# A Mamba and mixture-of-experts layer on one core: experts' copies and Silu ahead of the unit's Silu and softplus, norms turned a step later, routing operands in PSUM

## The chip, the cores and the metric

One core of a Trainium2 chip runs the kernel. The metric is the device time in microseconds (us) of one execution. The kernel before was timed three times: 1050.92, 1051.12 and 1053.75 us, median 1051.12. One further execution was profiled; all rows below are from it.

## The reference

The input x is 8 batches of 512 tokens of width 128. It is normalised once (`xn`), and the output is x plus two branches of `xn`:

```python
x = x + attn_ref(xn, ...) + ffn_ref(xn, ...)
# attn_ref: xn2 = layernorm(xn); for each direction d in (f, b):
xi, z = split(xn2 @ in_w.T);  xi = silu(conv4(xi) + conv_b)
dt, Bm, Cm = split(xi @ x_w.T, [8, 24])
delta = softplus(dt @ dt_w.T + dt_b)
h = h * exp(delta * A) + (delta * xi) * Bm      # 512 steps, 256 channels x 16 states
y = (sum(h * Cm) + xi * D) * silu(z);  out_d = y @ out_w.T
# attn = concat(out_f, out_b) @ combine_w.T + combine_b + xn
# ffn_ref: each token goes to expert e = argmax(xn @ router_w.T), of 8 experts
g = xe @ gate_w[e].T; u = xe @ up_w[e].T; ye = (silu(g) * u) @ down_w[e].T   # 352 wide
```

## The kernel before

**Units and steps.** A unit is one batch in one direction, so there are 16 units (`UNITS`). A unit has 16 steps (`NSTEP`), and 256 steps (`LAST`) make the scan; a few more follow. Each engine has its own program, and each program walks the same step numbers m in a loop written out by hand. What an engine does in a step stands in the order of the source. Engines meet through semaphores only, so a wait in one engine's step holds everything that stands behind it on that engine.

**The scan.** DVE does in an even step the product with B (`du_B`, line 997, 2048 elements a partition) and in the following odd step the linear recurrence (`scan`, lines 1015 and 1017). For the product of step m+1, PE first spreads `delta*xi` over partitions into `in_b` (`spread_du`, line 553); this stands first in PE's odd step m, behind all of PE's step m-1. ACT makes the decays `dA` four steps ahead (`decay(m + LEAD)`, line 847). POOL multiplies by C (line 1246), PE sums the states into the bank Y seven and eight steps later (`sum_states`, line 577).

**The front of a unit.** The projections of unit v are made during the unit before it, at fixed distances from its first step 16v. On PE: `in_proj` at -16 to -13, `x_proj` at -11, `dt_proj` at -10 and -9, `z_proj` at -7 and -6. On ACT: `keep_xi(v,0)` at -14; at step 16v-12, here called the Silu step, the load of the Silu table, `keep_xi(v,1)`, `silu(v)` (lines 791 and 794, xi of unit v and z of unit v-1) and the load of the exp table; `dbc_out` at -10; `dt_out` and `softplus` at -9 and -8; `keep_z` at -6 and -5. `x_proj` waits for the Silu, `dt_proj` for `dbc_out`. Softplus is computed as two activations of the exp and ln set; Silu lives in another set, and every change of set is a load of a table on ACT. Copies, Identity, Relu and Abs run under either set.

**Norms and routing.** In steps -3 to 26, ACT normalises the batches (`norm_one(c)` at 3c), PE turns each (`turn_xn`, 3c+2), ACT copies it out of the bank M (`turned_xn`, 3c+3), PE makes the router's logits in M (`router`, 3c+4) and ACT keeps them (`keep_logits`, 3c+5). `turn_xn(c)` waits until `keep_logits(c-1)` has left M. In step 27 (`R0`) DVE runs `route()`, 21 small instructions between a product with B and its recurrence: argmax by comparison, a prefix count with one pair of PE matmuls in the middle, positions and the expert of each tile. After it POOL scatters the tokens (32 indirect DMAs, steps 30 to 46).

**Experts.** 39 tiles of 128 sorted tokens follow, one each 3.75 steps, in steps 44 to 204 (`tiles_at(m, k)` gives the tiles whose stage k falls in step m). Per tile: PE gate matmuls (k=8, line 702) and the turn of the next tile; ACT at k=9 loads the Silu table (line 938), makes `th_f` = silu(gate) (line 943), loads the exp table (line 944) and copies `xsT` (line 948); PE at k=10 does the down matmuls of two tiles ago (line 634) and the up matmuls (line 639); ACT at k=11 copies `up_f` and, for two tiles ago, `ys` (lines 927 and 932). The gate matmuls wait for `up_f` of the tile before and for `ys`. In the tail, from step 207, POOL gathers the experts' rows back (32 indirect DMAs).

The Silu steps of units 1 to 16 are 4, 20, 36, ..., 244. Stage k=9 of a tile falls in the Silu steps 68, 116 and 180, and in the step after it for 52, 100 and 164. Stage k=11 falls in the Silu steps 100 and 148. ACT reads and refills the bank Y (`next_y`, lines 825 and 829) in steps with m % 8 = 5, that is also in the step after every Silu step.

## Time and profile before

| what | us |
|---|---|
| median of 3 executions | 1051.12 |
| the profiled execution | 1057.89 |
| its span in the trace | 1054.4 |
| DVE busy | 902.9 (86%) |
| POOL busy | 831.8 (79%) |
| PE busy | 812.2 (77%) |
| ACT busy | 741.2 (70%) |
| mean granted clock of TensorE | 0.887 of full speed |

Times in the rows count from the start of the span. A timeline row gives start, duration, engine, source line, operation and, in brackets, how long the engine had been idle before it and what ended that; "issue" means that the trace shows no releaser. PEld is the loading of weights beside the matmuls.

### The profile page before, as it was taken

Reading aid. Unit: us, or ns where it says so; the run is one execution under the profiler, and the core shown is the slowest. Engines: PE = TensorE matmul, PEld = TensorE weight load, DVE = VectorE, ACT = ScalarE, POOL = GpSimd, SP = SyncE. Lnnn points to the kernel's source line nnn. Section 1 sums busy time; section 2 is a strip of 40 time slices with the busy share of each in tenths; the row PEclk is TensorE's granted clock in tenths of the full one; section 3 lists DMA queues with packets and bytes.
Section 4 is the critical chain, followed back from the end, with each engine's and each line's share of the span. In section 5 each row is a group of like instructions: output and inputs, shape, how many; then the busy total and the mean of one; then the engine's idle time right before and its main releaser. Section 6 shows DMA issues by size and latency. Waiting matters only on the chain. (4 is left out here: it accounts for less than half of the span.)

```text
span 1054.4 us, 10031 instructions
## 1 busy us (share of the span) xinstructions
PE 812.2 (77%) x2887; PEld 326.5 (31%) x2887; DVE 902.9 (86%) x370; ACT 741.2 (70%) x1179; POOL 831.8 (79%) x474
## 2 busy tenths in 40 slices
PE   5777856755888897878988897887988887675556
PEld 2322311122233433424333443424324231112112
DVE  4789799956899988978999897977989999999696
ACT  3877744715798879797899879878888858465420
POOL 0288657889987969768797978877787889999992
PEclk9868997887899999899999998989989999788787
DMA  5676260252444526344364545433264433425200
GB/s 185 175 227 157 70 183 21 83 160 70 134 142 117 152 73 190 92 146 108 85 187 110 159 109 155 128 136 102 76 178 95 136 83 111 107 64 167 72 5 10
DMA packets 91303, 125.50 MB, mean 119 GB/s; under 512 B 8041, under 2 KB 62698, under 8 KB 87154
## 3 DMA queue, kind: packets, MB, share of 16 engines
q1 hardware_dynamic: 88464, 120.15, 40.4%
q0 software_dynamic: 2048, 4.20, 1.3%
q10 hardware_dynamic: 738, 0.53, 0.2%
q8 instruction: 23, 0.38, 0.1%
q14 instruction: 30, 0.25, 0.1%
HBM read 75.44 MB, written 16.38 MB: 87 GB/s over the span
## 5 line engine op out<-in xcount | busy, mean ns | idle before, releaser
L1246 POOL TENSOR_TENSOR hs<-hs,C_rep 128x1024 f32<-128x1024 f32 x253 | 593.3, 2361 | 186.6 <-DVE hs L1015 105.5
L847 ACT ACTIVATE dA<-delta_rep,A_sb 128x511 f32<-128x511 f32 x512 | 335.6, 715 | 83.7 <-DVE hs L1017 46.0
L997 DVE TENSOR_TENSOR in_b<-in_b,B_rep 128x2048 f32<-128x2048 f32 x128 | 294.3, 2299 | 108.1 <-PE in_b L553 92.7
L577 PE MATMUL y<-hs,cst 128*32 128x512 f32 x1024 | 277.4, 674 | 56.4 <-POOL hs L1246 56.4
L1015 DVE TENSOR_TENSOR_SCAN hs<-dA,in_b 128x2048 f32<-128x2048 f32 x64 | 282.9, 4421 | 8.5
L1017 DVE TENSOR_TENSOR_SCAN hs<-dA,in_b 128x2048 f32<-128x2048 f32 (+1 forms) x65 | 283.0, 4355 | 8.3
L553 PE MATMUL in_b<-du,cst 128*128 128x512 f32 x256 | 155.7, 696 | 25.4 <-DVE hs L1017 22.5
L515 PE MATMUL front<-xpad,w_in 128*128 128x512 f32 x248 | 125.3, 630 | 11.2 <-ACT xi L778 7.2
L577 PEld LDWEIGHTS y<-hs,cst 128*32 128x32 f32 x1024 | 55.9, 120 | 245.9 <-issue 195.5
L778 ACT ACTIVATE xi<-front,cols 128x512 f32<-128x512 f32 x30 | 20.6, 687 | 79.0 <-PE front L515 79.0
L553 PEld LDWEIGHTS in_b<-du,cst 128*128 128x128 f32 x256 | 46.1, 209 | 93.9 <-issue 91.7
L515 PEld LDWEIGHTS front<-xpad,w_in 128*128 128x128 f32 x248 | 44.7, 196 | 82.4 <-issue 65.4
L634 PE MATMUL moe<-dn_w,th_f 128*128 128x128 f32 x234 | 38.0, 304 | 36.2 <-issue 36.2
L546 PE MATMUL front<-dbc,w_dt 8*128 8x512 f32 x62 | 40.4, 735 | 25.3 <-ACT dbc L801 25.2
L634 PEld LDWEIGHTS moe<-dn_w,th_f 128*128 128x128 f32 x234 | 33.3, 209 | 62.7 <-issue 62.7
L944 ACT ACT_TABLE_LOAD x39 | 50.0, 1283 | 0.7
L528 PE MATMUL front<-xpad,w_in 128*128 128x512 f32 x62 | 36.0, 664 | 18.1 <-ACT zs L784 18.0
L938 ACT ACT_TABLE_LOAD x36 | 46.2, 1283 | 0.6
L825 ACT COPY yg<-y 128x512 f32<-128x512 f32 x31 | 17.8, 574 | 35.8 <-PE y L577 35.8
L702 PE MATMUL moe<-xsT,gu_w 128*128 128x128 f32 x234 | 37.0, 298 | 7.3 <-ACT ys L932 7.3
L702 PEld LDWEIGHTS moe<-xsT,gu_w 128*128 128x128 f32 x234 | 32.8, 205 | 30.0 <-issue 30.0
L639 PE MATMUL moe<-xsT,gu_w 128*128 128x128 f32 x234 | 36.5, 298 | 7.0 <-ACT xsT L948 7.0
(131 smaller groups left out, 845.2 us busy)
## 6 DMA issues: line engine op xcount, KB each, us to landing
delta_rep<-tmpA SPq DMA_DIRECT2D x126, 256.0 KB, 4.4
B_rep<-dbc_scratch SPq DMA_DIRECT2D x16, 1024.0 KB, 5.1
C_rep<-dbc_scratch SPq DMA_DIRECT2D x16, 1024.0 KB, 7.4
gu_w<-in_gate_up SPq DMA_DIRECT2D x39, 384.0 KB, 3.5
dn_w<-in_down SPq DMA_DIRECT2D x39, 192.0 KB, 2.4
xs<-sorted_tokens SPq DMA_DIRECT2D x39, 64.0 KB, 3.0
sorted_ffn<-ys SPq DMA_DIRECT2D x39, 64.0 KB, 1.6
sorted_tokens<-up_f SPq DMA_DIRECT2D x9, 256.0 KB, 3.6
```

What stands on the lines that cost most here:

```text
L515: i = e.matmul((M if v == 0 and h else F)[:, :], w_in[:, d, k, h * P:(h + 1) * P], xpad[:, at:at + L], start=(k == 0), stop=(k == NTAP - 1))
L553: e.matmul(in_b[:, R * (j % 2), :], spread(j), du[:, du_slot(v, j // 4), :], start=True, stop=True).then_inc(pe_du, 1)
L577: i = e.matmul(Y[c * DD:(c + 1) * DD, :], sel, hs[:, (m + 2 * w + rh) % NH, r * L:(r + 1) * L], start=False, stop=(rh == 1 and r == RH - 1 ...
L634: i = e.matmul(M[:, IFP:IFP + H], th_f[:, (n - 2) % 3, c * P:(c + 1) * P], dn_w[:, (n - 2) % ND, c, :], start=(c == 0), stop=(c == NCH - 1))
L702: i = e.matmul(M[:, c * P:(c + 1) * P], gu_w[:, w, 0, c * P:(c + 1) * P], xsT[:, n % 2, :], start=True, stop=True)
L847: i = e.activation(dA[:, m // 2 % NA, r * L + 1:(r + 1) * L], src, ACT.Exp, scale=A_sb[:, d, 2 * p + jj, r:r + 1])
L938: e.preload_act_table_set(SILU_SET)
L944: e.preload_act_table_set(EXP_SET)
L997: e.tensor_tensor(to, in_b[:, R * (s // 2 % 2), :].unsqueeze(1).broadcast_to([P, R, L]), by, ALU.mult).then_inc(dve_mult, 2)
L1015: e.tensor_tensor_scan(to, a[:, first:first + n], b, 0.0, ALU.mult, ALU.add).then_inc(dve_scan, done)
L1017: e.tensor_tensor_scan(to[:, ::-1], a[:, first + 1:first + n + 1][:, ::-1], b[:, ::-1], 0.0, ALU.mult, ALU.add).then_inc(dve_scan, done)
L1246: e.tensor_tensor(hs[:, m % NH, :], hs[:, m % NH, :], C_rep[:, u % 2, RH * rh:RH * rh + RH, :].rearrange("p r t -> p (r t)"), ALU.mult).th ...
```

## The change

It has four parts, and leaves what is computed as it is.

1. **Order on ACT.** In a step the copies out of the banks come first (also `dbc_out` and `dt_out`), then the experts' copies, the experts' Silu and `xsT`, then `keep_xi(v,1)`, `next_y`, `decay(m + 4)`, and behind the decays `softplus` and, in a Silu step, the load of the Silu table, `silu(v)` and the load of the exp table. Where an expert's Silu falls in the Silu step itself, `silu(v)` runs right after it under the same table, ahead of `next_y` and the decays.
2. **Table loads.** The exp table is not loaded between a Silu step and an expert's Silu in the next one (52, 100, 164), nor the Silu table again: 98 loads in the loop instead of 104.
3. **Norms.** `turn_xn` and `turned_xn` come a step later (3c+3, 3c+4). `router(c)` stays in step 3c+4, but goes to the end of PE's step, behind the projections; `keep_logits` stays.
4. **Routing.** In step 26 ACT copies the logits and the numbers 0 to 7 into the bank M, and the comparison reads them there; the rank is written to and read from M. After the matmuls the two copies out of M are gone, and scan, sum and difference read M. `route()` has 19 instructions instead of 21, and one wait more (`act_route`).

```diff
@@ PE @@
-                for c in norms(m, 3):
+                for c in norms(m, 4):
                     turn_xn(c)
-                for c in norms(m, 5):
-                    router(c)
...
+                for c in norms(m, 5):
+                    router(c)
                 if m == R0:
-                    e.wait_ge(dve_route, N_PREFIX - 1)
+                    e.wait_ge(dve_route, N_ONE)
@@ ACT @@
             for m in range(STEPS):
+                silu_next = [v for v in range(1, UNITS + 1) if front_step(v, -12) == m]
+                gate_next = tiles_at(m, 9)
...
-                for v in range(1, UNITS + 1):
-                    if front_step(v, -12) == m:
-                        e.preload_act_table_set(SILU_SET)
-                        if v < UNITS:
-                            keep_xi(v, 1)
-                        silu(v)
-                        if not tiles_at(m, 9):
-                            e.preload_act_table_set(EXP_SET)
                 for v in fronts(m, -10):
                     dbc_out(v)
                 for v in fronts(m, -9):
                     dt_out(v, 0)
-                    softplus(v, 0)
                 for v in fronts(m, -8):
                     dt_out(v, 1)
-                    softplus(v, 1)
...
-                for c in norms(m, 4):
+                for c in norms(m, 5):
                     turned_xn(c)
...
-                if m % 8 == 5 and 0 <= m // 8 - 1 < 2 * UNITS - 1:
-                    next_y(m // 8 - 1)
+                if m == R0 - 1:
+                    e.wait_ge(act_logits, NB)
+                    e.copy(M[:, 0:256], logits[:, :, :].rearrange("p k e -> p (k e)")).then_inc(act_route, 1)
+                    e.copy(M[:, 256:512].rearrange("p (k e) -> p k e", e=E),
+                           cst[:, C_IOTA:C_IOTA + E].unsqueeze(1).broadcast_to([P, NBLK, E])).then_inc(act_route, 1)
...
-                for n in tiles_at(m, 9):
-                    if (m + 12) % NSTEP:
+                for n in gate_next:
+                    if (m + 11) % NSTEP or tiles_at(m - 1, 9):
                         e.preload_act_table_set(SILU_SET)
...
                     e.activation(th_f[:, n % 3, :], M[:, 0:IFP], ACT.Silu).then_inc(act_thf, 1)
-                    e.preload_act_table_set(EXP_SET)
+                    if not silu_next:
+                        e.preload_act_table_set(EXP_SET)
...
+                for v in silu_next:
+                    if v < UNITS:
+                        keep_xi(v, 1)
+                    if gate_next:
+                        silu(v)
+                        e.preload_act_table_set(EXP_SET)
+                if m % 8 == 5 and 0 <= m // 8 - 1 < 2 * UNITS - 1:
+                    next_y(m // 8 - 1)
                 if m + LEAD < LAST:
                     decay(m + LEAD)
+                for v in fronts(m, -9):
+                    softplus(v, 0)
+                for v in fronts(m, -8):
+                    softplus(v, 1)
+                for v in silu_next:
+                    if not gate_next:
+                        e.preload_act_table_set(SILU_SET)
+                        silu(v)
+                        if not tiles_at(m + 1, 9):
+                            e.preload_act_table_set(EXP_SET)
@@ DVE, route() @@
+                e.wait_ge(act_route, 2)
-                e.tensor_tensor(val.rearrange(ke, e=E), logits[:, :, :],
+                e.tensor_tensor(val.rearrange(ke, e=E), M[:, 0:256].rearrange(ke, e=E),
                                 best.unsqueeze(2).broadcast_to([P, NBLK, E]), ALU.is_ge).then_inc(dve_route, 1)
-                e.scalar_tensor_tensor(val.rearrange(ke, e=E), val.rearrange(ke, e=E), -float(E), iota,
+                rank = M[:, 0:256].rearrange(ke, e=E)
+                e.scalar_tensor_tensor(rank, val.rearrange(ke, e=E), -float(E), M[:, 256:512].rearrange(ke, e=E),
                                        ALU.mult, ALU.add).then_inc(dve_route, 1)
-                e.tensor_tensor(one.rearrange("p (e k) -> p k e", e=E), val.rearrange(ke, e=E),
+                e.tensor_tensor(one.rearrange("p (e k) -> p k e", e=E), rank,
                                 low.unsqueeze(2).broadcast_to([P, NBLK, E]), ALU.is_equal).then_inc(dve_route, 1)
                 e.wait_ge(pe_route, 1)
-                e.tensor_copy(cnt, M[:, 256:512]).then_inc(dve_route, 1)
-                e.tensor_copy(pref, M[:, 0:256]).then_inc(dve_route, 1)
-                e.wait_ge(dve_route, 7)
-                e.tensor_tensor_scan(cum, cst[:, C_NOTFIRST:C_NOTFIRST + 256], cnt, 0.0,
+                e.tensor_tensor_scan(cum, cst[:, C_NOTFIRST:C_NOTFIRST + 256], M[:, 256:512], 0.0,
                                      ALU.mult, ALU.add).then_inc(dve_route, 1)
```

## Rows read from the trace of the kernel before

**Rows 1.** groups by line (busy us, mean ns, idle before)

```profile
L1246 POOL TENSOR_TENSOR hs<-hs,C_rep 128x1024 f32<-128x1024 f32 x253 | 593.3, 2361 | 186.6 <-DVE hs L1015 105.5 <-DVE hs L1017 79.8
...
L997 DVE TENSOR_TENSOR in_b<-in_b,B_rep 128x2048 f32<-128x2048 f32 x128 | 294.3, 2299 | 108.1 <-PE in_b L553 92.7 <-DMA C_rep<-dbc_scratch 4.4 <-DVE hs L1015 0.5
...
L944 ACT ACT_TABLE_LOAD x39 | 50.0, 1283 | 0.7
```

**Rows 2.** busy time by stretch: PE, PEld, DVE, ACT, POOL, PEclk, DMA share, GB/s

```profile
156.50:262.00 105.50, 63.98 (x177) 20.60 (x177) 80.35 (x25) 46.92 (x74) 90.29 (x61) 0.77 0.29 82
...
262.00:843.00 581.00, 493.54 (x1936) 216.19 (x1937) 515.91 (x155) 490.81 (x768) 477.54 (x259) 0.94 0.45 128
...
843.00:1054.00 211.00, 142.12 (x445) 45.70 (x443) 185.83 (x59) 100.42 (x155) 179.10 (x107) 0.83 0.29 77
```

**Rows 3.** waits: DVE from 35 to 142, DVE 262 to 843, POOL 843 to 1000

```profile
DVE in_b L997 <- PE in_b L553: 10.6, 5, 3.8
...
DVE in_b L997 <- PE in_b L553: 55.4, 33, 6.9
...
POOL hs L1246 <- DVE hs L1015: 2.7, 2, 2.3
```

**Rows 4.** timeline of DVE during routing (start us, us, what)

```profile
143.19 1.39 DVE L1048 TENSOR_TENSOR gu_w<-logits,small 128x256 f32<-128x256 f32 x1
...
144.62 1.37 DVE L1051 SCALAR_TENSOR_TENSOR gu_w<-gu_w,cst 128x256 f32<-128x256 f32 x1
...
146.48 2.15 DVE L1056 TENSOR_TENSOR gu_w<-gu_w,small 128x256 f32<-128x256 f32 x1
...
149.86 0.42 DVE L1059 COPY gu_w<-moe 128x256 f32<-128x256 f32 x1 [1.22 <-PE moe L688]
...
150.20 0.41 DVE L1060 COPY gu_w<-moe 128x256 f32<-128x256 f32 x1
...
151.37 0.42 DVE L1065 TENSOR_TENSOR gu_w<-gu_w 128x256 f32<-128x256 f32 x1
```

**Rows 5.** timeline of POOL during routing

```profile
145.67 2.52 POOL L1246 TENSOR_TENSOR hs<-hs,C_rep 128x1024 f32<-128x1024 f32 x1
```

**Rows 6.** timeline of PE and DVE before routing

```profile
59.20 1.09 PE L478 MATMUL moe<-cst,xn 128*128 128x128 f32 x4 [4.34 <-ACT logits L756]
...
68.69 2.30 DVE L997 TENSOR_TENSOR in_b<-in_b,B_rep 128x2048 f32<-128x2048 f32 x1 [1.11 <-PE in_b L553]
...
78.62 2.30 DVE L997 TENSOR_TENSOR in_b<-in_b,B_rep 128x2048 f32<-128x2048 f32 x1 [3.08 <-PE in_b L553]
...
123.69 1.09 PE L478 MATMUL moe<-cst,xn 128*128 128x128 f32 x4 [2.62 <-ACT logits L756]
...
126.57 2.30 DVE L997 TENSOR_TENSOR in_b<-in_b,B_rep 128x2048 f32<-128x2048 f32 x1 [3.84 <-PE in_b L553]
```

**Rows 7.** timeline of ACT, PE and DVE around step 100

```profile
449.88 0.69 ACT L778 ACTIVATE xi<-front,cols 128x512 f32<-128x512 f32 x1 [1.72 <-PE front L515]
...
454.88 1.62 PE L702 MATMUL moe<-xsT,gu_w 128*128 128x128 f32 x6 [3.19 <-ACT ys L932]
...
458.25 2.30 DVE L997 TENSOR_TENSOR in_b<-in_b,B_rep 128x2048 f32<-128x2048 f32 x1 [5.72 <-PE in_b L553]
```

**Rows 8.** timeline of PE and DVE after step 164

```profile
699.67 1.23 PE L634 MATMUL moe<-dn_w,th_f 128*128 128x128 f32 x6 [4.63 <-issue]
...
706.28 2.30 DVE L997 TENSOR_TENSOR in_b<-in_b,B_rep 128x2048 f32<-128x2048 f32 x1 [5.58 <-PE in_b L553]
```

**Rows 9.** timeline of PE and DVE after step 52

```profile
279.19 1.62 PE L639 MATMUL moe<-xsT,gu_w 128*128 128x128 f32 x6 [4.67 <-ACT xsT L948]
...
284.96 2.30 DVE L997 TENSOR_TENSOR in_b<-in_b,B_rep 128x2048 f32<-128x2048 f32 x1 [4.14 <-PE in_b L553]
```

**Rows 10.** timeline of ACT in step 109

```profile
486.55 0.59 ACT L825 COPY yg<-y 128x512 f32<-128x512 f32 x1 [4.00 <-PE y L577]
...
488.52 0.59 ACT L919 COPY xnT<-front 128x512 f32<-128x512 f32 x1 [0.66 <-PE front L596]
```

More of the change, by code:

```diff
@@ L249, in mamba_moe_kernel @@
         act_first, act_thf, act_xsT, act_ys = sem("act_first"), sem("act_thf"), sem("act_xsT"), sem("act_ys")
+        act_route = sem("act_route")
         act_y, act_D, act_up, act_out = sem("act_y"), sem("act_D"), sem("act_up"), sem("act_out")
@@ L1040, in route @@
             def route():
-                one, val, pref, cnt, cum, tmp = (scratch(i) for i in range(6))
+                one, val, pref, cum, tmp = (scratch(i) for i in range(5))
                 ke, ek = "p (k e) -> p k e", "p (e k) -> p e k"
-                iota = cst[:, C_IOTA:C_IOTA + E].unsqueeze(1).broadcast_to([P, NBLK, E])
                 best, low = small[:, 0:32], small[:, 32:64]
@@ L1071, in route @@
                 e.tensor_tensor(tmp.rearrange(ek, e=E), total, thr, ALU.is_gt).then_inc(dve_route, 1)
-                e.wait_ge(dve_route, 11)
+                e.wait_ge(dve_route, 9)
                 ntile, end, first = small[:, 0:E], small[:, E:2 * E], small[:, 2 * E:3 * E]
                 e.tensor_reduce(ntile, tmp.rearrange(ek, e=E), AX_X, ALU.add).then_inc(dve_route, 1)
+                e.wait_ge(dve_route, 10)
+                e.tensor_tensor_scan(end, ones[:, 0:E], ntile, 0.0, ALU.mult, ALU.add).then_inc(dve_route, 1)
+                e.wait_ge(dve_route, 11)
+                e.tensor_tensor(first, end, ntile, ALU.subtract).then_inc(dve_route, 1)
                 e.wait_ge(dve_route, 12)
-                e.tensor_tensor_scan(end, ones[:, 0:E], ntile, 0.0, ALU.mult, ALU.add).then_inc(dve_route, 1)
-                e.wait_ge(dve_route, 13)
-                e.tensor_tensor(first, end, ntile, ALU.subtract).then_inc(dve_route, 1)
-                e.wait_ge(dve_route, 14)
                 e.scalar_tensor_tensor(
```

29 lines of the change are left out of this document (14 added, 15 removed).

## The prediction

> **What bounds the kernel now.** I read four views, in this order. The groups by line show what each step costs on DVE, and what ended the idle time before its product with B: of 108.1 us, 92.7 end with PE's spreading matmul, `spread_du` [rows 1]. So DVE's own rate is the floor, and what stands above it is PE coming late. The busy time by stretch shows that this differs by stage. While POOL scatters (156 to 262 us) POOL is busy 90.29 of 105.5 us; in the experts' stage (262 to 843) DVE is busy 515.91 and ACT 490.81 of 581; in the tail (843 on) POOL leads [rows 2]. The waits by stretch give the prize: DVE waits 10.6 us for PE before routing and 55.4 us in the experts' stage, while POOL waits only 2.7 us for DVE from 843 to 1000 [rows 3]. So in the scatter and in the tail POOL sets the pace, and an order on ACT costs or gives nothing there; whatever is gained ahead of them moves them forward whole. Last, the timelines around DVE's gaps say why PE was late: it stood at its queue's head for ACT. Before routing it waited 4.34 and 2.62 us to turn a norm until the logits were kept, and the products behind began 1.11, 3.08 and 3.84 us late [rows 6]. Around step 100 it waited 3.19 us for `ys`, which stood behind the Silu, and the product came 5.72 late [rows 7]. After the Silu steps 164 and 52 it waited 4.63 and 4.67 us for the expert's Silu and `xsT`, and the products came 5.58 and 4.14 late [rows 8, 9].
>
> **Part 1, routing: -4.0 us.** Nothing but these small instructions runs on DVE's path here, so each counts in full. Three instructions with two operands in SBUF took 1.39, 1.37 and 2.15 us, while one with 256 elements and two SBUF operands took 0.42 later [rows 4]. The difference: POOL was working beside the first three (its product from 145.67 covers most of the 2.15, and itself took 2.52 us instead of the mean 2.361) [rows 1, 5]. A copy out of a bank took 0.42 [rows 4]. No row shows a two-operand instruction of this size with one operand in PSUM while POOL works, so bounds: 0.42 (the bank's copy, the quiet SBUF one) to 1.39. The large product with B reads a bank and SBUF all the time beside POOL, and its mean 2299 ns for 2048 elements is 1.12 ns each [rows 1], which is nearest to 0.42; I take it. That gives 0.97 and 0.95. The third also writes with a stride, so I give it 1.3 of its possible 1.73. The two copies out of M go: from 149.86 to 150.20 and 0.41 more, 0.8 us. Sum 4.0, bounds 0.8 and 4.5. ACT's two added copies in step 26 are of 256 elements, less than the 0.59 of a 512 one [rows 10]; the logits are there before DVE's product ends, so the new wait should find them done, and if ACT were late they would cost up to 1.0.
>
> The Trainium skill speaks against this part: "VectorE: DVE Perf Modes", section "Rules for kernel authors", says of elementwise work on matmul output to accept the slow mode or to copy to SBUF first if many operations follow. Here fp32 two-operand work showed no faster mode in SBUF (0.42 against the copy's 0.42), so I see no price for it in the rows.
>
> **Part 2, norms: -4.8 us.** `turn_xn` now follows `spread_du` of the odd step or has a step more for the logits, so the waits of 4.34 and 2.62 us leave PE's queue [rows 6]. The gaps 1.11 and 3.08 close, 4.2 us. What is late next: `router` now stands behind `z_proj` in step 10, where it used to run in that one's wait, 0.8 back. One more gap of 1 us, behind `turn_xn(4)`, closes: 10.6 in five pieces less the three shown leaves 2.6 for two [rows 3, 6], and the other is PE's own dense work. The last, 3.84 at 126.57 [rows 6], mostly comes back: `dt_proj(2,0)` waits for `dbc_out`, ACT has no room there, and the Silu table's load no longer hides in a wait; 0.4 stays. Sum 4.2 - 0.8 + 1.0 + 0.4 = 4.8. Bounds 0 and 9.6 (10.6 less 1). No DMA moves; SP's stores of xn wait for `norm_one`, which now needs `turn_xn` of PE's same step, some microseconds ahead of it.
>
> **Part 3, the Silu step with an expert's Silu right behind (52, 100, 164): -7.5 us.** Count ACT's queue from `keep_xi(v,1)` to `xsT`. Gone: two table loads, 2 x 1.283 = 2.57 [rows 1], and `next_y`, 1.31 (488.52 - 0.66 - 486.55) [rows 10], which goes behind. Added: the Silu table's load, which used to run while `keep_xi` waited for PE (1.72 us still waited after it at 449.88 [rows 7]) and now stands behind the decays in full, 1.28. So `xsT` is 2.6 us earlier; `dbc_out`, which has `next_y` ahead of it in both orders, 1.3. PE needs both before `spread_du`. PE needs less time after a shorter wait, too: behind the waits of 3.19, 4.63 and 4.67 us six small matmuls took 1.62, 1.23 and 1.62 us [rows 7 to 9], and the same engine does more per microsecond in the dense stage, where its clock is 0.94 [rows 2]; as an estimate that is 0.9 and 1.6. So I take 2.2 for step 52 (of 4.14) and 2.9 for 164 (of 5.58) [rows 8, 9]. At 100 the wait for `ys` goes (3.19), the gap of 5.72 falls by 4.3 [rows 7], but `dt_proj` then waits for `dbc_out` and 1.9 comes back: 2.4 stays. Bounds 3 (only 1.3 twice) and 15.4 (all three gaps).
>
> The Trainium skill, "ScalarE: Activation LUTs", section "What ACT_TABLE_LOAD costs", gives 1283 ns and a drain of 1380 for every change of set. The first is the row's number; the second doesn't show, since the 39 loads have 0.7 us of idle before them in all and what follows them starts at once. By that rule the three places would be worth 3 x 2 x 1.38 = 8.3 us more.
>
> **Part 4, the other Silu steps: +4.4 us.** With no expert's Silu in the next step nothing is saved, but the table's load has left its shadow, 1.28 each time PE holds up `keep_xi`; `x_proj` and `dbc_out` are later by it. This matters where DVE already stood for PE a few steps later: 84, 148 (0.9, as `up_f` and `ys` fill the wait), 180 (0.9) and 196, together 1.3 + 0.9 + 0.9 + 1.3. In 68, 116 and 132 there is slack; 36 lies in the scatter, 212 to 244 in the tail, where POOL's rate covers it [rows 2]. Cover gone, each would cost 1.3 too.
>
> **Part 5, `next_y` behind the rest: +4.3 us.** In step 109 it ran inside ACT's wait for the output matmuls (4.00 us before it, only 0.66 left after it) [rows 10]; now it stands behind them, ahead of the second norm that `turn_x` waits for. 1.31 each in 77, 109, 141, 173, less the slack DVE has at 109 and 173 (0.4 each): 4.3. The queue behind it, decays, then norm; who waits is PE's `turn_x`, then `spread_du`.
>
> **Part 6, softplus behind the decays: 0.** POOL waits for it. It comes 1.3 us later (two activations of 512 change places with a decay), and POOL stood 2.7 us in all for DVE late and much more before [rows 1, 3]; from 0 to +3.
>
> **Sum.** -4.0 - 4.8 - 7.5 + 4.4 + 4.3 = -7.6 us. The profiled execution took 1057.89 (span 1054.4); it becomes 1050.3. It was 6.8 above the median 1051.12, so the median becomes 1043.5.
>
> **Rivals.**
> - *Given back.* Only routing's 4 us survives: the gains of parts 2 and 3 meet ACT's or PE's next dense stretch, as the 3.84 did, and just cover parts 4 and 5. 1051.1 - 4.0 = 1047. For it: ACT is busy 84% in the experts' stage [rows 2].
> - *More.* PE's waits vanish and with them its slow clock (0.94 of full in the experts' stage, 0.77 in the scatter) [rows 2]: parts 2 and 3 near their bounds, -9.6 - 12 - 4 + 4.5 = -21: 1030. The page's 8.3 us more would give 1035, inside this.
> - *Slower: ACT's lost shadows.* 13 Silu steps have the table's load behind the decays and 7 steps have `next_y` behind the output copy, 20 places x 1.29 = 25.8 us if none has slack, against 16.3 of gains: +9.5, 1060.6. It decides from 13 of the 20 places on (16.3 / 1.29); I count 8. Against it: POOL covers 7 of them.
> - *Routing doesn't gain.* A PSUM operand doesn't spare DVE from POOL: only the copies' 0.8 goes, 1046.7. This is the page's side of part 1.
>
> **Chances.** Forecast 0.45, given back 0.2, more 0.2, slower 0.1, routing 0.05. Its own range is 1038 to 1049 from the bounds of parts 2 and 3 taken half; to leave out no more than 2 in 10 I take 1030 to 1055. A measurement of this kernel can tell 0.3%, about 3.2 us, from no change; so faster means below 1047.9. Faster: 0.42 + 0.09 (of 0.2, since 1047 lies just at the edge) + 0.2 + 0.03 = 0.74; slower 0.12 (the rival and a little of what is given back); within 0.3%, 0.14.
>
> **What would show each step.** Routing: the three comparisons at 0.4 to 0.5 us (the third under 1.2), no copies, no wait for `act_route`. Norms: PE's waits for the logits near 0, the first four gaps of DVE gone, a new one behind 126 us. Part 3: no product more than 3 us late after steps 52, 100 and 164, 98 table loads in the loop. Parts 4 and 5: products 1 to 2 us later after 84, 148, 196, and 77 to 173, with PE waiting longer for `dbc` and the second norm. The prediction is wrong if DVE's waits for PE in the experts' stage stay at 55 us or rise, or if POOL waits for softplus.

## The result and the profile after

The changed kernel takes 1059.01 us (median of 5 executions, 1058.06 to 1060.16), where the kernel before, on the same chip, takes 1051.12 (5 executions, 1050.42 to 1054.16). The ratio is 1.0064, 95% interval 1.0045 to 1.0083. So it is slower by 0.64%, where 1043.5 us was predicted, with a range of 1030 to 1055. The profiled execution took 1059.85 us (span 1057.7) and lies near its median, while that of before stood 6.8 us above its own. So the two traces differ by 3.3 us only, where the medians differ by 7.9; they say nothing of the rest.

The groups by line of the changed kernel answer [rows 1] (busy us, mean ns, idle before). DVE waits longer for PE: 99.6 us instead of 92.7. The five lines with table loads in the loop add up to 98 loads where they were 104. The one shown has 36 instead of 39 only because, in the three steps where the unit's Silu and an expert's fall together, the load stands on another line now:

```profile
L1012 DVE TENSOR_TENSOR in_b<-in_b,B_rep 128x2048 f32<-128x2048 f32 x128 | 294.3, 2299 | 114.1 <-PE in_b L554 99.6
...
L941 ACT ACT_TABLE_LOAD x36 | 46.2, 1283 | 0.6
```

Busy time by stretch of the changed kernel, as in [rows 2] (PE, PEld, DVE, ACT, POOL, PEclk, DMA share, GB/s): in the experts' stage ACT is busy 10 us less, 480.75 against 490.81, and the stage takes 585 us where it took 581.

```profile
262.00:847.00 585.00, 491.62 (x1944) 213.94 (x1943) 517.04 (x155) 480.75 (x763) 479.47 (x259) 0.94 0.45 128
```

The waits of the changed kernel say who is late: first DVE from 35 to 147 us, then DVE, PE and POOL from 262 to 847.

```profile
DVE in_b L1012 <- PE in_b L554: 14.7, 5, 6.1
...
DVE in_b L1012 <- PE in_b L554: 57.9, 33, 6.0
...
PE front L547 <- ACT dbc L802: 25.4, 10, 3.9
PE front L529 <- ACT zs L785: 12.6, 8, 2.2
PE front L497 <- ACT xn L730: 12.3, 4, 4.4
...
POOL tmpA L1192 <- ACT tmpB L817: 16.1, 8, 3.3
```

Before, the first two were 10.6 and 55.4 [rows 3], and in the same stage PE waited 12.6 us for `dbc`, 10.2 for `zs`, 8.5 for the second norm, and POOL 3.0 for softplus. The waits that the change aimed at did get shorter: PE's for `ys` from 7.3 to 3.6 us and for `xsT` from 7.0 to 2.0. The waits for `dbc`, `zs` and the second norm grew by more.

**Routing**: the small instructions got faster as predicted. DVE and POOL of the changed kernel, against [rows 4, 5]; the kernel with routing alone has the same 0.42, 0.43 and 0.62 us with POOL busy beside all of them:

```profile
147.98 0.42 DVE L1063 TENSOR_TENSOR gu_w<-moe,small 128x256 f32<-128x256 f32 x1 [0.36 <-ACT moe L906]
148.44 0.43 DVE L1067 SCALAR_TENSOR_TENSOR moe<-gu_w,moe 128x256 f32<-128x256 f32 x1
...
149.36 0.62 DVE L1072 TENSOR_TENSOR gu_w<-moe,small 128x256 f32<-128x256 f32 x1
...
147.17 1.27 POOL L1197 TENSOR_TENSOR du<-tmpA,xi 128x512 f32<-128x512 f32 x1
148.40 2.36 POOL L1259 TENSOR_TENSOR hs<-hs,C_rep 128x1024 f32<-128x1024 f32 x1
```

But the whole stretch, from the product of step 26 to that of step 28, became only 2.65 us shorter (17.87 for 20.52). DVE now waits 0.31 us for the logits, 0.36 for the copies in the bank M and 2.08 for the prefix count, where it waited 1.22 for the count alone.

**Norms** didn't. PE no longer waits for the logits, but two larger gaps stand in the place of [rows 6]. The timeline of SP, ACT, PE and DVE of the changed kernel:

```profile
67.63 0.53 SPq L356 DMA_DIRECT2D B_rep<-dbc_scratch  x1
68.20 0.60 SPq L356 DMA_DIRECT2D C_rep<-dbc_scratch  x1
68.85 0.59 SPq L331 DMA_DIRECT2D xn_scratch<-xn  x1
...
77.64 1.65 ACT L730 ACTIVATE xn<-attn_in,shift,rstd 128x128 f32<-128x128 f32 x4 [4.32 <-issue]
...
79.81 2.08 PE L529 MATMUL front<-xpad,w_in 128*128 128x512 f32 x2 [7.65 <-ACT zs L785]
...
85.39 2.30 DVE L1012 TENSOR_TENSOR in_b<-in_b,B_rep 128x2048 f32<-128x2048 f32 x1 [3.90 <-PE in_b L554]
...
119.45 0.18 ACT L757 COPY logits<-moe 128x32 f32<-128x32 f32 x1 [3.01 <-PE moe L485]
...
130.70 2.07 PE L547 MATMUL front<-dbc,w_dt 8*128 8x512 f32 x2 [4.92 <-ACT dbc L802]
...
136.58 2.30 DVE L1012 TENSOR_TENSOR in_b<-in_b,B_rep 128x2048 f32<-128x2048 f32 x1 [6.13 <-PE in_b L554]
```

`norm_one(3)` is next on ACT and waits 4.32 us. The view names no releaser, but the norm overwrites `xn`, whose store (L331) landed 8.6 us after its issue, at about 77.5, behind two loads of 1 MB. Before, that store landed at about 77.3 and ACT came to the norm only at 79.72, so nothing waited for it. The trace of f4, one of the kernels below, names the releaser of the same wait:

```profile
76.29 1.65 ACT L730 ACTIVATE xn<-attn_in,shift,rstd 128x128 f32<-128x128 f32 x4 [4.42 <-DMA xn_scratch<-xn]
```

The second gap, at step 24, has a cause in ACT's new order too. In step 20, which is a Silu step, the copies out of the banks come first, so ACT idles 3.01 us for the router's product (L485) ahead of `keep_xi` and the unit's Silu. `dbc_out` is late by it, and PE waits 4.92 us. With ACT's order of before and the same norms (e4 below) this gap is 2.95 us, not 6.13.

**The three Silu steps** 52, 100 and 164 went about as predicted where they stand. DVE of the changed kernel after each, against [rows 9], [rows 7] and [rows 8]: gaps of 2.29, 0.51 and none, for 4.14, 5.72 and 5.58.

```profile
283.79 2.30 DVE L1012 TENSOR_TENSOR in_b<-in_b,B_rep 128x2048 f32<-128x2048 f32 x1 [2.29 <-PE in_b L554]
...
463.79 2.30 DVE L1012 TENSOR_TENSOR in_b<-in_b,B_rep 128x2048 f32<-128x2048 f32 x1 [0.51 <-PE in_b L554]
...
708.84 2.30 DVE L1012 TENSOR_TENSOR in_b<-in_b,B_rep 128x2048 f32<-128x2048 f32 x1
```

Laid side by side product for product, the changed kernel gains 5.6 us at step 102 and 5.5 at step 168 and loses them again, mostly in the steps 8 and 10 of other units (88, 90, 120, 122, 136, 154, 184, 200) and at 144, behind a `next_y`. **next_y** lost its cover: ACT in step 109 of the changed kernel, against [rows 10], now stands 6.23 us for the output matmuls with nothing to do, and refills Y after it.

```profile
487.62 0.59 ACT L915 COPY xnT<-front 128x512 f32<-128x512 f32 x1 [6.23 <-PE front L597]
...
491.48 0.59 ACT L826 COPY yg<-y 128x512 f32<-128x512 f32 x1
```

### The profile page after: what moved, and what is told of

Same layout as the page of the kernel before. It is cut to its first block and busy times, and to the rows that moved or that the text cites. A ratio compares the mean times of both kernels' runs of the same rounds, so it can differ in the third digit from the quotient of the medians.

```text
span 1057.7 us, 10026 instructions
## 1 busy us (share of the span) xinstructions
PE 815.1 (77%) x2887; PEld 327.0 (31%) x2887; DVE 898.7 (85%) x368; ACT 730.2 (69%) x1175; POOL 831.4 (79%) x474
## 5 line engine op out<-in xcount | busy, mean ns | idle before, releaser
L1012 DVE TENSOR_TENSOR in_b<-in_b,B_rep 128x2048 f32<-128x2048 f32 x128 | 294.3, 2299 | 114.1 <-PE in_b L554 99.6
L578 PE MATMUL y<-hs,cst 128*32 128x512 f32 x1024 | 280.4, 680 | 53.0 <-POOL hs L1259 53.0
L554 PE MATMUL in_b<-du,cst 128*128 128x512 f32 x256 | 153.5, 687 | 20.3 <-DVE hs L1032 19.9
L1192 POOL TENSOR_TENSOR tmpA<-tmpA,tmpB 128x512 f32<-128x512 f32 x30 | 38.1, 1270 | 16.1 <-ACT tmpB L817 16.1
L538 PE MATMUL front<-xi,w_x 128*40 128x512 f32 x64 | 33.3, 647 | 13.8 <-ACT xi L792 13.5
L810 ACT ACTIVATE tmpA<-front,cols 128x512 f32<-128x512 f32 x31 | 21.2, 682 | 30.5 <-PE front L547 30.5
L1204 POOL TENSOR_TENSOR yg<-yg,zs 128x512 f32<-128x512 f32 x31 | 39.3, 1267 | 2.7 <-ACT yg L826 2.7
```

Source lines behind the costliest of these rows:

```text
L554: e.matmul(in_b[:, R * (j % 2), :], spread(j), du[:, du_slot(v, j // 4), :], start=True, stop=True).then_inc(pe_du, 1)
L578: i = e.matmul(Y[c * DD:(c + 1) * DD, :], sel, hs[:, (m + 2 * w + rh) % NH, r * L:(r + 1) * L], start=False, stop=(rh == 1 and r == RH - 1 ...
L1012: e.tensor_tensor(to, in_b[:, R * (s // 2 % 2), :].unsqueeze(1).broadcast_to([P, R, L]), by, ALU.mult).then_inc(dve_mult, 2)
L1204: e.tensor_tensor(yg[k], yg[k], zs[k], ALU.mult).then_inc(pool_gated, 1)
```

## The experiments

All kernels were timed in alternation with the kernel before, whose median moved between 1051.1 and 1053.1 us; so kernels are compared by their ratios. A difference of ratios is turned into time at 1052 us, so 0.001 is 1.05 us. Each ratio has an interval of about 2 us to either side, so a difference of two is known to about 3 us.

| kernel | median us | ratio to before | 95% interval |
|---|---|---|---|
| changed kernel | 1059.01 | 1.0064 | 1.0045 to 1.0083 |
| e1 routing alone | 1054.45 | 1.0012 | 0.9991 to 1.0033 |
| e2 norms alone | 1054.70 | 1.0009 | 0.9994 to 1.0024 |
| e3 ACT's order and loads alone | 1059.46 | 1.0067 | 1.0042 to 1.0093 |
| e4 routing and norms | 1049.76 | 0.9977 | 0.9958 to 0.9996 |
| f1 changed, softplus back | 1062.35 | 1.0093 | 1.0072 to 1.0114 |
| f2 changed, next_y back | 1052.00 | 0.9989 | 0.9975 to 1.0003 |
| f3 changed, ten Silus back | 1053.78 | 1.0013 | 0.9999 to 1.0027 |
| f4 changed, all three back | 1047.75 | 0.9957 | 0.9941 to 0.9973 |
| g1 changed, next_y and ten Silus back | 1048.79 | 0.9961 | 0.9942 to 0.9979 |
| g2 f4, and three Silus back | 1062.06 | 1.0103 | 1.0083 to 1.0123 |
| g3 e4 and next_y's move | 1056.79 | 1.0047 | 1.0032 to 1.0062 |
| g4 g1 and router ahead | 1046.73 | 0.9940 | 0.9913 to 0.9967 |
| h1 e4 and the three steps | 1042.06 | 0.9902 | 0.9883 to 0.9921 |
| h2 h1, router and store ahead | 1048.18 | 0.9967 | 0.9948 to 0.9985 |
| h4 changed, Silus of 68, 116, 180 back | 1056.43 | 1.0038 | 1.0024 to 1.0053 |
| h5 changed, store of xn ahead | 1055.26 | 1.0032 | 1.0017 to 1.0048 |
| i1 before and the three steps | 1045.79 | 0.9954 | 0.9930 to 0.9977 |
| i2 h1 and store of xn ahead | 1040.79 | 0.9893 | 0.9871 to 0.9914 |

### Which part costs

e1 takes only the routing of the diff, e2 only the two steps of the norms and the router's place, e3 only the order and loads on ACT, e4 routing and norms. Their edits are those parts of the diff shown with the change:

```diff
# e1 and e4
+                if m == R0 - 1:
+                    e.wait_ge(act_logits, NB)
+                    e.copy(M[:, 0:256], ...).then_inc(act_route, 1)
# e2 and e4
-                for c in norms(m, 3):
+                for c in norms(m, 4):
                     turn_xn(c)
# e3
+                silu_next = [v for v in range(1, UNITS + 1) if front_step(v, -12) == m]
+                gate_next = tiles_at(m, 9)
```

> The kernel before with part 4 alone (routing reads the bank M). In the traces of the two kernels the stretch from the last product before routing (step 26) to the first one behind it (step 28) is 20.5 us before and 17.9 us after. If routing gains by itself and everything behind it moves forward whole: 2.6 us faster than before, 1048.5. If the scatter behind it, where POOL sets the pace, eats the gain: within 1 us of before.

> The kernel before with the norms' part alone (turn and copy a step later, router at the end of PE's step). Theory A, the norms cost: in the trace of the changed kernel norm_one(3) stood 4.3 us on ACT for something that is no engine's, the transfers of xn, and PE waited 7.7 us behind it; the gain of 4.0 us at step 10 is 0.2 at step 12. Then 0 to +2 us against before. Theory B, the norms gain and only ACT's new order took it back (dbc later at step 24): 2 to 4 us faster than before.

> The kernel before with ACT's new order and the six table loads saved, norms and routing as before. Theory A, the order is what costs: the changed kernel is 7.9 us slower though routing gives 2.6, so the order costs 8 to 11 us alone: 1059 to 1062. Theory B, the norms cost and the order is neutral: within 2 us of before.

> The kernel before with norms and routing of the change, ACT's order as before. If the parts add up: the sum of the two runs alone; theory A 1048 to 1051, that is 8 to 11 us faster than the changed kernel; theory B (norms cost) 1055 or more.

e3 alone has the whole loss (+7.0 us; the change has +6.7), so the loss lies in ACT's order, and routing and norms, -2.4 together, didn't add their gain to it. They are worth less than my 8.8 even on the order of before. They don't add either: alone they come out at +1.3 and +0.9 us, together at -2.4, which is somewhat more apart than the noise explains; why is open.

In e1's trace 4.1 us are gained between the products of step 26 and 28 (16.43 us, before 20.52), and 3.6 of them are still there at the last step; its median doesn't show them. The stretch itself is not to blame: the four traces with the old routing (before, e2, e3, i1) have 19.91 to 20.52 us there. So the two traces are no typical pair for the rest: from step 50 to 204, where before, e1, e2 and e4 run the same instructions, their traces take 582.6, 584.5, 582.6 and 578.2 us. With the norms a step later, the stretch is 17.87 to 18.03 us wherever the router stands behind the projections, so next to the norms routing gains 2.5 of the 4.1.

e2's trace leads by 2.12 us at step 10 and by 1.57 at step 12, gains 3.7 more at step 22, loses 1.3, 1.0, 2.5 and 1.3 at steps 16, 18, 24 and 26, and is level from step 28 on. The store's landing costs it little (a gap of 0.68 at step 12).

### The three moves on ACT, one by one

Each puts one thing back in the changed kernel: f1 the softplus to its place behind `dt_out`; f2 `next_y` ahead of the output copy and the experts' copies; f3 the Silu ahead of the decays in the ten Silu steps that have no expert's Silu in the same or the next step, with the table's load in front of `keep_xi`; f4 all three.

```diff
# f1
                     dt_out(v, 0)
+                    softplus(v, 0)
...
                     dt_out(v, 1)
+                    softplus(v, 1)
# f2
+                if m % 8 == 5 and 0 <= m // 8 - 1 < 2 * UNITS - 1:
+                    next_y(m // 8 - 1)
                 if m == R0 - 1:
# f3
+                early = bool(silu_next) and not gate_next and not tiles_at(m + 1, 9)
+                    if early:
+                        e.preload_act_table_set(SILU_SET)
...
-                    if gate_next:
+                    if gate_next or early:
                         silu(v)
```

> The changed kernel with softplus back right behind dt_out, ahead of the decays. Theory A1, softplus behind the decays is the cost (POOL waits 16.1 us for it in the experts' stage, 3.0 before): 5 us or more faster than the changed kernel, 1054 or less. Theory A2, it is the unit's Silu behind the decays, whose late xi and dbc hold PE (its waits for dbc rose from 12.6 to 25.4 us there): within 2 us of the changed kernel, 1059.

> The changed kernel with next_y back ahead of the output copy and the experts' copies. Part 5 of the prediction priced its move at 4.3 us. Right: 3 to 5 us faster than the changed kernel, 1054 to 1056. If the shadow was worth nothing: 1059.

> The changed kernel with the unit's Silu ahead of next_y and the decays again, its table loaded in the wait of keep_xi, in the 10 Silu steps that have no expert's Silu in the same or the next step; 52, 100 and 164 stay as changed. Theory A2: PE's waits for dbc and for xi fall back and the kernel is 4 to 8 us faster than the changed one, 1051 to 1055. Theory A1 or next_y: within 2 us of it.

> The changed kernel with softplus, next_y and those 10 Silus all back. What stays of the new order is the experts' copies ahead of the Silu and steps 52, 100 and 164 with 98 table loads. If the three moves are the whole cost and part 3 of the prediction (7.5 us of gain) holds: 1043 to 1046, against 1050 for the kernel with routing and norms alone. If part 3 gains nothing: 1050. If the cost lies in part 3 itself: 1056 or more.

Against the changed kernel f2 gives 7.9 us back (I had 4.3), f3 5.4 (of my 4.4, 3.5 belong to these ten steps), and f1 loses 3.1: in the changed kernel the late softplus is no loss and perhaps a gain. f4 is 4.5 us faster than before, only 2.1 more than e4. So what is left of the ACT edits, the three steps with the kept table, looked as if they were worth 2 us and not 7.5.

### What the three steps are worth, and the price of next_y alone

g1 is f4 with the softplus left late. g2 is f4 with the Silu ahead of the decays in 52, 100 and 164 too, and all tables loaded. g3 is e4 with `next_y` moved ahead of the decays. g4 is g1 with `router` ahead of the projections again.

```diff
# g2, against f4
-                    if (m + 11) % NSTEP or tiles_at(m - 1, 9):
+                    if True:
                         e.preload_act_table_set(SILU_SET)
...
-                early = bool(silu_next) and not gate_next and not tiles_at(m + 1, 9)
+                early = bool(silu_next) and not gate_next
# g3, against e4
-                if m % 8 == 5 and 0 <= m // 8 - 1 < 2 * UNITS - 1:
-                    next_y(m // 8 - 1)
...
+                if m % 8 == 5 and 0 <= m // 8 - 1 < 2 * UNITS - 1:
+                    next_y(m // 8 - 1)
                 if m + LEAD < LAST:
                     decay(m + LEAD)
# g4, against g1
                 for c in norms(m, 4):
                     turn_xn(c)
+                for c in norms(m, 5):
+                    router(c)
```

> The changed kernel with next_y and the Silus of its ten odd steps put back ahead, and the softplus left behind the decays. Theory A (the order of ScalarE's work costs, and each move has its own price): the softplus behind the decays is worth the 3.3 us that it was worth in the changed kernel (1062.35 against 1059.01), so this run gives 1043 to 1046 us, under the 1047.75 of the kernel with all three back. Theory B (the softplus helps only where the Silu and next_y stand late beside it): 1047 to 1050 us.

> The kernel with all three back (1047.75 us), in which steps 52, 100 and 164 also get the unit's Silu ahead of the decays and the tables loaded as before; only the experts' copies stay ahead. My prediction had the three steps at 7.5 us: then this run gives 1055 us. If the traces are right that 5.6 us are gained at step 100 and 5.5 us at step 164 and mostly given back at the next steps, it gives 1049 to 1051 us. At 1047 to 1048 the three steps are worth nothing.

> The kernel of routing and norms alone (1049.76 us) with one move more: next_y behind the experts' Silu and ahead of the decays, as the change has it. If next_y costs by itself what it cost in the changed kernel (7 us), or what I predicted (4.3 us), this run gives 1054 to 1057 us. If it costs only beside the late Silu and softplus, 1050 to 1051 us.

> As the run with next_y and the Silus back, but the router of a tile stands ahead of the projections again, while the norms stay a step later. My prediction priced the router behind z_proj at 0.8 us a place: then this run is 1 to 2 us faster than that one. If the stalls there are the transposes' and the norm's own, it is equal to it within 1 us, or slower, as the router then waits for the transposes itself.

**g3** costs 7.4 us over e4, as much as in the changed kernel, so `next_y`'s price stands by itself. Product for product its four places have 1.1 us at step 80, 2.3 at 112, 1.0 at 144 and 2.3 at 176, 6.7 together; elsewhere in the experts' stage the two traces drift apart and back by up to 2.6 us. The timelines around step 176 say why it is more than the 1.31 us of `next_y` there. First g3, ACT and PE, then DVE; then the same of e4:

```profile
730.28 0.59 ACT L923 COPY xnT<-front 128x512 f32<-128x512 f32 x1 [6.39 <-PE front L597]
...
734.15 0.59 ACT L826 COPY yg<-y 128x512 f32<-128x512 f32 x1
...
736.62 1.63 ACT L730 ACTIVATE xn<-xn,shift,rstd 128x128 f32<-128x128 f32 x4
...
738.31 1.11 PE L497 MATMUL front<-cst,xn 128*128 128x128 f32 x4 [1.32 <-ACT xn L730]
739.22 1.91 PE L554 MATMUL in_b<-du,cst 128*128 128x512 f32 x2
...
741.23 2.30 DVE L1003 TENSOR_TENSOR in_b<-in_b,B_rep 128x2048 f32<-128x2048 f32 x1 [2.40 <-PE in_b L554]
```

```profile
722.77 0.59 ACT L925 COPY xnT<-front 128x512 f32<-128x512 f32 x1 [0.66 <-PE front L597]
...
727.87 1.64 ACT L730 ACTIVATE xn<-xn,shift,rstd 128x128 f32<-128x128 f32 x4
...
729.56 0.66 PE L497 MATMUL front<-cst,xn 128*128 128x128 f32 x4 [1.15 <-ACT xn L730]
730.05 1.02 PE L554 MATMUL in_b<-du,cst 128*128 128x512 f32 x2
...
731.45 2.30 DVE L1003 TENSOR_TENSOR in_b<-in_b,B_rep 128x2048 f32<-128x2048 f32 x1
```

From the copy `xnT` to the norm it is 6.34 us in g3 and 5.10 in e4: 1.24 more, the `next_y`. From PE's turn of the norm to the product it is 2.92 us in g3 and 1.89 in e4: 1.03 more, the clock. TensorE's granted clock in those 4 us was 0.57 of full in g3 and 1.00 in e4, near its lower (1.2 GHz) and at its higher level (2.4 GHz).

But the late `next_y` doesn't by itself bring the slow clock. In g3 it fell at 735 us, ahead of PE's wait for the late norm and behind a wait of 2.46 us that e4 has too. Seven traces have `next_y` behind (the changed kernel, e3, f1, f3, g3, h4 and h5); at step 176 five of them keep the full clock, and there the place costs 1.1 us. The changed kernel, PE and DVE, and its clock:

```profile
739.02 0.66 PE L497 MATMUL front<-cst,xn 128*128 128x128 f32 x4 [2.38 <-ACT xn L730]
...
740.63 2.30 DVE L1012 TENSOR_TENSOR in_b<-in_b,B_rep 128x2048 f32<-128x2048 f32 x1 [1.08 <-PE in_b L554]
...
736.50:740.50 4.00, 1.62 (x10) 0.73 (x10) 3.05 (x1) 4.00 (x9) 2.39 (x3) 1.00 0.22 66
```

In all seven the gap of this product is either 1.1 us, at a clock of 1.00, or 2.4, at 0.50 (g3 and f1). At step 112 it is 1.1 in two of them and 2.4 in five. So a place costs about the `next_y` itself, and twice that where the clock is low; which of the two it gets isn't decided by the move alone.

**g2** is 15.4 us slower than f4. So the three steps are worth far more than 2 us in that kernel, outside all that was expected, and something else in the ACT order must take it away. At step 104, for one, g2 has a gap of 6.52 us that the kernel before doesn't have. g1 equals f4 (0.4 us apart), so the softplus's 3.1 us are not a price of its own. g4 is 2.2 us faster than g1, inside the uncertainty.

### What ate the three steps

The timelines at step 116 showed a candidate. In the Silu steps 68, 116 and 180, here called the joint steps, an expert's Silu falls in the same step. The change puts it first, and with it its wait for the gate matmuls. ACT, PE and DVE of f4:

```profile
508.57 0.49 ACT L943 ACTIVATE th_f<-moe 128x384 f32<-128x384 f32 x1 [3.23 <-PE moe L703]
...
509.90 1.06 ACT L792 ACTIVATE xi<-xi 128x1024 f32<-128x1024 f32 x1
...
516.90 0.56 ACT L802 COPY dbc<-front 40x512 f32<-40x512 f32 x1
517.52 2.07 PE L547 MATMUL front<-dbc,w_dt 8*128 8x512 f32 x2 [2.96 <-ACT dbc L802]
521.69 2.30 DVE L1013 TENSOR_TENSOR in_b<-in_b,B_rep 128x2048 f32<-128x2048 f32 x1 [2.81 <-PE in_b L554]
```

ACT idles 3.23 us in front of the expert's Silu and so of `keep_xi`; the unit's Silu and so `x_proj` and `dbc_out` are later, PE waits 2.96 for `dbc`, goes on at a clock of 0.52 (2.07 us for two matmuls), and DVE stands 2.81.

h1 is e4 with the three steps alone (`late` holds the unit of a Silu step 52, 100 or 164) and that order left as it was; h4 takes that order alone back in the changed kernel. h5 puts the store of `xn` ahead of the loads of B and C on SP, in the changed kernel; h2 is h1 with router and store ahead.

```diff
# h1, against e4
-                    if front_step(v, -12) == m:
+                    if front_step(v, -12) == m and not tiles_at(m + 1, 9):
...
-                    if (m + 12) % NSTEP:
+                    if (m + 12) % NSTEP and ((m + 11) % NSTEP or tiles_at(m - 1, 9)):
...
+                for v in late:
+                    if v < UNITS:
+                        keep_xi(v, 1)
                 if m + LEAD < LAST:
                     decay(m + LEAD)
+                for v in late:
+                    e.preload_act_table_set(SILU_SET)
+                    silu(v)
# h4, against the changed kernel
+                if gate_next:
+                    for v in silu_next:
+                        e.preload_act_table_set(SILU_SET)
+                        if v < UNITS:
+                            keep_xi(v, 1)
+                        silu(v)
                 for n in gate_next:
# h5, against the changed kernel; h2 has it too
+                for c in norms(m, 2):
+                    store_norm(c)
                 for v in fronts(m, -9):
                     load_bc(v)
```

> Routing and norms (1049.76 us) with the late Silu and the kept table in steps 52, 100 and 164 alone; ScalarE's order is that of before everywhere else, so in steps 68, 116 and 180 the unit's Silu is again ahead of the expert's. Theory A (the expert's Silu, waiting for its gate product ahead of the unit's chain in those three steps, is what ate the gain): 1038 to 1042 us, as the three steps are worth 8 to 12 us without it. Theory B (a stall removed in step 100 or 164 only moves to the next steps, whatever the order): 1047 to 1049 us, the time with all three put back (1047.75).

> The run with the three steps alone, and the router ahead of the projections, and the store of xn ahead of the loads of B and C in SP's order. If the router's place is worth the 2.1 us that it was in the run before and the store's 2 to 4 us of the gap at step 12, this run is 3 to 6 us faster than the run with the three steps alone. If the norms' stalls only move to step 24, it is 0 to 2 us faster.

> The changed kernel (1059.01 us) with one edit: in steps 68, 116 and 180 the unit's keep_xi and Silu stand ahead of the expert's Silu again, as before the change. Theory A: 1050 to 1055 us (4 to 9 us less; the traces show 3.7 us at steps 120 to 124 and 0 at 72 and 184, so the lower gain is likelier). Theory B: 1058 to 1060 us.

> The changed kernel (1059.01 us) with one edit: in step 7 the store of xn stands ahead of the loads of B and C in SP's order (so in every step where both fall). If norm_one of step 9 waits for that store's landing, as the trace shows (issued at 68.85, landed at 77.49 us, behind two loads of 1 MB), it starts at about 73.5 instead of 77.6 us and the gap of 3.9 us at step 12 goes: 1055 to 1057 us, and the trace shows the step 12 product some 3 to 4 us earlier. If ScalarE is late for another reason the gap stays at 3 us or more.

**h1** is 7.9 us faster than e4 and 10.3 faster than before. At the same place (ACT, PE and DVE of h1) the chain is short, and the clock in 515.5 to 519.5 is 1.00:

```profile
507.64 1.06 ACT L792 ACTIVATE xi<-xi 128x1024 f32<-128x1024 f32 x1
...
509.55 0.47 ACT L949 ACTIVATE th_f<-moe 128x384 f32<-128x384 f32 x1
...
515.19 0.56 ACT L802 COPY dbc<-front 40x512 f32<-40x512 f32 x1
515.80 1.12 PE L547 MATMUL front<-dbc,w_dt 8*128 8x512 f32 x2 [0.69 <-ACT dbc L802]
518.12 2.30 DVE L1010 TENSOR_TENSOR in_b<-in_b,B_rep 128x2048 f32<-128x2048 f32 x1
```

h4 prices the joint steps alone: in the changed kernel their order costs 2.7 us, about the least that two ratios can tell, and less than expected. PE's waits for `dbc` fall to 18.6 us there, from 25.4; h1 has 13.3. f4 is 5.8 us slower than h1, but it differs from h1 in every Silu step, since in f4 the unit's Silu stands behind all copies out of the banks. Product for product f4 loses 3.7 us at steps 120 and 122 and 2.3 at 184 and 186, behind joint steps, and also 3.0 at step 12 (the wait for the store) and 3.7 at step 24 (the wait for the router's product), where no expert is near; part of it is won back elsewhere. So the theory that the order of the joint steps ate the gain holds in part: the same fault, a wait for PE or for a store ahead of work that PE needs, stands at steps 9 and 20 as well.

**h5** confirms the store: in its trace the norm starts at 73.06 and the gap at step 12 is gone, and the kernel is 3.4 us faster. (The traced execution of h5 was the slowest of its twelve, 1060.43 us; it serves for the place and not for the time.)

```profile
73.06 1.63 ACT L730 ACTIVATE xn<-attn_in,shift,rstd 128x128 f32<-128x128 f32 x4
...
81.47 2.30 DVE L1012 TENSOR_TENSOR in_b<-in_b,B_rep 128x2048 f32<-128x2048 f32 x1
```

**h2** was expected to be faster than h1 and is 6.8 us slower. Two runs settle whether the store or the router is to blame, and what the three steps are worth on the kernel before. i1 has the edit of h1 on before; i2 the edit of h5 on h1.

```diff
# i2, against h1
+                for c in norms(m, 2):
+                    store_norm(c)
                 for v in fronts(m, -9):
                     load_bc(v)
```

> The kernel before with the late Silu and the kept table in steps 52, 100 and 164 alone. If the three steps add to the rest, they are worth here what they are on top of routing and norms, 7.7 us (1042.06 against 1049.76), near the 7.5 us of my prediction: 1043 to 1046 us where before has 1051 to 1052.5. If they gain only where routing and norms have shifted the steps: 1049 us or more.

> The run with the three steps alone on routing and norms (1042.06 us), and the store of xn ahead of the loads of B and C, but the router where the change has it. If the store's place was worth its 3.8 us of the changed kernel here too: 1038 to 1040 us, and the loss of the run that had both moved lies in the router's place. If the store ahead is what cost: 1046 to 1049 us. With neither by itself: 1041 to 1043 us.

i2 is the fastest kernel of the study, 1040.79 us, 1.1% under before. The store's move is worth 0.9 us there by the ratios, which can't be told from nothing; h1 had a gap of only 0.70 at step 12, against 3.90 in the changed kernel. h2 differs from i2 in nothing but the router's place and is 7.8 us slower, so that place is what cost h2. Its trace shows most of it in DVE's routing: the logits and the count come late, 2.35 and 4.12 us, where the changed kernel has 0.31 and 2.08, and the stretch from the product of step 26 to that of 28 takes 21.94 us for i2's 18.03.

```profile
144.78 0.42 DVE L1058 TENSOR_REDUCE small<-logits 128x32 f32<-128x256 f32 x1 [2.35 <-ACT logits L757]
...
151.66 0.69 DVE L1073 TENSOR_TENSOR_SCAN gu_w<-cst,moe 128x256 f32<-128x256 f32 x1 [4.12 <-PE moe L689]
```

g4 has the same place of the router and lost nothing by it (18.87 us in that stretch, for g1's 17.88). So the place costs 7.8 us with ACT's order of before in most steps and nothing that can be measured with most of the new one; why stays open. i1 is 4.8 us faster than before (interval 2.4 to 7.4), and DVE's gap after step 100, 5.72 before, is 0.54 in its trace.

## Why the prediction was wrong, point by point

The kernels e4 and h1 split the way to the changed kernel in three: routing and norms -2.4 us (I had -8.8), the three Silu steps -7.9 (I had -7.5), and all that the order on ACT costs beside them +17.0 (I had +8.7). So two steps of the prediction failed: the gains of parts 1 and 2, and the price of the new order.

- **Part 1, routing, -4.0.** Mechanism right in the rows: 0.42, 0.43 and 0.62 us where I took 0.42, 0.42 and 0.85; alone, the stretch is 4.1 shorter. An operand in PSUM did spare DVE from POOL. The step that failed is "nothing but these small instructions runs on DVE's path here, so each counts in full". In the changed kernel only 2.65 of it arrive, since DVE waits there for the logits, the bank and the count. And in the median e1 is 1.3 us slower than before, interval -0.9 to +3.5, which excludes a gain of 4 us. Where it went isn't shown, since one execution of each kernel is traced, and that of before stood 6.8 us above its median.
- **Part 2, norms, -4.8.** The waits for the logits left PE and the gaps at steps 8 and 10 closed, as predicted. The failed step is what comes back. The gap of 1 us at step 16 was to close and is 2.33 in e2, the one at step 18 grew from 1.57 to 2.58, and e2 is +0.9 and not -4.8. "No DMA moves" failed in the changed kernel: none did, but ACT came earlier to a norm that waits for a store's landing; the time that ACT used to waste had covered it. Gap 3.90 at step 12, confirmed by h5. The gap at 126 us, of which 3.4 was to stay, is 2.61 and 2.95 in e2 and e4, at step 24, so near that; it is 6.13 with ACT's new order. Measured for parts 1 and 2: -2.4 instead of -8.8.
- **Part 3, 52, 100 and 164, -7.5.** Right in size: -7.9 on e4, -4.8 on before, which the noise allows to be the same. The working is not shown to be right: it counted `next_y`'s 1.31 us among what leaves the queue, and h1 and i1 leave `next_y` where it was. At 100 the gap falls by 5.1 in h1 (I had 4.3) and 3.2 come back at steps 104 and 108 (I had 1.9). And I counted only their queue, and priced "the experts' Silu first" nowhere else.
- **Part 4, +4.4.** 3.5 of it belonged to three of the ten steps (84, 148, 196) and 0.9 to step 180. For the ten steps 5.4 was measured, which is 3.5 within the noise. What failed is the price of 68, 116 and 180, slack in the first two and 0.9 in the third: the Silu there doesn't only lose the load's shadow, it stands behind a wait for the gate matmuls. That is 2.7 us by h4. Not priced at all was that `keep_xi` and the Silu now stand behind the norms' copies, which is a wait of 3.01 us at step 20.
- **Part 5, next_y, +4.3.** The place and the mechanism were right, the size was 7.4 to 7.9. (Four times 1.31 less 0.8 is 4.4 and not 4.3.) I took off slack of 0.4 at 109 and 173, and the traces show at most 0.2. What was missing is TensorE's clock, which makes a place cost 2.4 instead of 1.1 us where it is low.
- **Part 6, softplus, 0 to +3.** In the changed kernel -3.1, about the least that two ratios can tell, and nothing in g1 (+0.4). POOL did wait for it (16.1 us instead of 3.0), which I had named as a sign of trouble; it was none. The cause of the 3.1 isn't settled.
- **The tail.** "In the tail POOL leads" is a wrong reading of [rows 2]: DVE is busy 185.83 us there and POOL 179.10. What was concluded from it holds: in all twenty traces the way from the product of step 204 to that of 254 takes 192.85 to 193.15 us, and from 28 to 50 97.5 to 99.0, whatever ACT's order.
- **Sum.** The moves add up within the noise along one path: -2.4 (e4), -7.9 (h1), +5.8 (f4), then +7.9, +5.4 and -3.1 make +5.7; measured +6.7. Between kernels they don't carry over exactly: routing and norms alone are not worth their -2.4 together, the store's place is worth 3.4 us in the changed kernel and 0.9 on h1, the router's nothing on g1 and 7.8 on i2.
- **Rivals.** The third, ACT's lost shadows (1060.6, chance 0.1), has the time and the sign, in part by luck: it set 25.8 us of costs against 16.3 of gains, where 17.0 and 10.3 came. `next_y` fits it, at up to 2.3 us a place instead of 1.29; the waits ahead of the Silu are not in it. "Given back" was right for the norms. The clause that it would be wrong if DVE's waits for PE stay at 55 us or rise came true: 57.9.
- **The drain that the Trainium skill gives for a change of set** ("ScalarE: Activation LUTs", "What ACT_TABLE_LOAD costs") shows no more than before: 0.6 us of idle before 36 loads. The three steps were worth 7.9 us and not 8.3 more. g2's 15.4 comes near to 7.5 and 8.3 together, but its 104 loads in the loop have 1.9 us of idle before them in all, so the trace shows no drain there either.

## What to carry to other kernels

A move that makes an in-order engine reach an instruction earlier must be priced with everything that instruction waits for, the landings of stores too. Don't put an instruction that waits for another engine ahead of a chain that the bounding engine stands for, even if it saves a table load; keep the saving where it is free. Work that ran inside a wait costs its own time once it is moved out, and up to as much again where TensorE's clock is low behind it; one trace doesn't tell how often that is.

## What was not expected of the hardware

- After waits of 3 to 8 us TensorE often ran at half clock for some microseconds: granted 0.52 in 517 to 521 us of f4, behind a wait of 2.96 us; 0.50 in 130 to 134 of the changed kernel, behind 4.92; and 0.50 in its 80 to 87, behind 7.65. The same wait doesn't always do it: PE waits 3.12 us for the norm ahead of the product of step 80 in before and in e4, and behind it the clock is 0.50 in 367 to 371 us of before and 1.00 in 362 to 366 of e4.

```profile
80.00:87.00 7.00, 7.00 (x18) 3.12 (x20) 3.10 (x2) 4.18 (x9) 7.00 (x5) 0.50 0.93 212
```

- A store of 256 KB issued behind two loads of 1 MB landed after 8.6 us in the changed kernel, and after 8.2 to 8.8 in all seventeen traces with that order; issued ahead of them, after 3.6 in h5 and 2.3 in i2.
- Three DVE instructions of 256 elements took 1.39, 1.37 and 2.15 us with both operands in SBUF beside POOL, and 0.42, 0.43 and 0.62 with one in PSUM.
